# A pad of 32 bytes in front of the row constants of a two-layer attention and feed-forward kernel

## What is computed

```python
x = x + L0_attn(layernorm(x))   # 16 heads, linear attention with phi = silu + 1:
                                # kv = phi(k)^T v per head, out = phi(q) kv, then Wo
x = x + L0_ffn(layernorm(x))    # ternary weights w1, w2, h1, h2, w3 with a scale per output:
                                # h = silu(x w1) * (x w2); h = gelu(h h1); h = gelu(h h2); h w3
x = x + L1_attn(layernorm(x))   # one head over 256 features, softmax over 512 keys
x = x + L1_ffn(layernorm(x))    # tanh(x weight aux1 aux2 + bias)
```

## Time and profile before

| | |
|---|---|
| median of 3 runs | 1983.38 us |
| span of the profiled execution | 1981.5 us, granted TensorE clock 0.996 on the mean |
| PE busy (matmul) | 1961.9 us, 99%, 15288 matmuls |
| VectorE busy | 1289.0 us, 65% |
| ScalarE busy | 1020.0 us, 51% |
| GpSimd busy | 406.8 us, 21% |
| DMA | 46.03 MB, nearly all in the first 100 us |

### The profile page before, as it was taken

One profiled execution on the slowest core, in us unless ns is written; L12 is line 12 of the kernel. 1 busy time (PEld: TensorE's weight loads), 2 busy tenths in 40 slices (PEclk: granted clock), 3 DMA queues, 4 the chain that ended last, 5 costly groups with the idle time before them and its releaser, 6 DMA issues.

```text
span 1981.5 us, 37810 instructions
## 1 busy us (share of the span) xinstructions
PE 1961.9 (99%) x15288; PEld 1895.6 (96%) x15288; DVE 1289.0 (65%) x3292; ACT 1020.0 (51%) x1786; POOL 406.8 (21%) x344
## 2 busy tenths in 40 slices
PE   8999999999999999999999999999999999999998
PEld 7999999999999999999999999999999999999996
DVE  6546768566685665767667676666856667676357
ACT  3445545555554655455554455555546454554433
POOL 1112212212122021311213121121220213112121
PEclk9999999999999999999999999999999999999999
DMA  9600000000000000000000000000000000000000
GB/s 359 224 3 1 22 1 12 11 2 22 1 22 1 1 22 1 22 1 1 22 1 22 1 1 22 1 22 1 23 1 1 22 1 12 1 1 12 1 1 23
DMA packets 24538, 46.03 MB, mean 23 GB/s; under 512 B 1264, under 2 KB 21488, under 8 KB 24176
## 3 DMA queue, kind: packets, MB, share of 16 engines
q1 hardware_dynamic: 24352, 43.41, 6.1%
HBM read 35.02 MB, written 19.92 MB: 28 GB/s over the span
## 4 chain that ended last, share of the span: by engine, by line
PE 97%; DMA 1%; DVE 1%; SPq 1%; issue 0%; ACT 0%; POOL 0%; DVEq 0%; ACTq 0%
PE ffn_fill L1117 49%; PE att_fill L1048 25%; PE ffn_fill L1048 13%; PE ffn_fill L1174 6%; PE att_fill L1136 1%; PE att_fill L1252 1%; DMA scratch_w2T<-in_w2T 1%; DMA w<-scratch_w1T 0%; SPq L543 0%; PE ffn_fill L1285 0%; DVE late_sm L869 0%; PE ffn_fill L1280 0%; ACT late_kv_b L1009 0%; DVE st L671 0%; DVE late_prob_t_lo L864 0%
## 5 line engine op out<-in xcount | busy, mean ns | idle before, releaser
L1117 PE MATMUL ffn_fill<-act_hi,h 128*128 128x256 f32 x4096 | 987.2, 283 | 0.8 <-issue 0.2
L1117 PE MATMUL ffn_fill<-act_lo,h 128*128 128x256 f32 x4096 | 978.2, 280 | 1.2 <-issue 1.2
L1117 PEld LDWEIGHTS ffn_fill<-act_hi,h 128*128 128x128 f32 x4096 | 770.3, 188 | 9.2 <-POOL act_lo L649 3.9
L1117 PEld LDWEIGHTS ffn_fill<-act_lo,h 128*128 128x128 f32 x4096 | 773.1, 189 | 3.6
L976 ACT ACTIVATE whole<-ffn_fill,scales 128x256 f32<-128x256 f32 x512 | 214.0, 469 | 291.3 <-PE ffn_fill L1117 290.1
L649 POOL TENSOR_TENSOR act_lo<-whole,act_hi 128x512 fp32r<-128x512 f32 x128 | 166.8, 1303 | 492.4 <-DVE act_hi L798 492.4
L802 DVE TENSOR_TENSOR act_lo<-whole,act_hi 128x512 fp32r<-128x512 f32 x256 | 183.4, 716 | 112.0 <-ACT act_hi L980 109.7
L1048 PE MATMUL ffn_fill<-half_hi,w 128*128 128x256 f32 x1024 | 245.9, 283 | 0.0
L1048 PE MATMUL ffn_fill<-half_lo,w 128*128 128x256 f32 x1024 | 244.3, 281 | 0.0
L1048 PEld LDWEIGHTS ffn_fill<-half_lo,w 128*128 128x128 f32 x1024 | 193.3, 189 | 0.1
L1048 PEld LDWEIGHTS ffn_fill<-half_hi,w 128*128 128x128 f32 x1024 | 192.5, 188 | 0.4 <-issue 0.2
(11 more groups left out here) (239 smaller groups left out, 3277.8 us busy)
## 6 DMA issues: line engine op xcount, KB each, us to landing
x<-in_L_attn_x SPq DMA_DIRECT2D x16, 512.0 KB, 3.3
out<-x SPq DMA_DIRECT2D x15, 512.0 KB, 2.9
h<-scratch_h1T SPq DMA_DIRECT2D x2, 2048.0 KB, 13.1
h<-scratch_h2T SPq DMA_DIRECT2D x2, 2048.0 KB, 13.4
w<-scratch_w1T SPq DMA_DIRECT2D x1, 1024.0 KB, 7.8
w<-scratch_w2T SPq DMA_DIRECT2D x1, 1024.0 KB, 9.8
w<-scratch_w3T SPq DMA_DIRECT2D x1, 1024.0 KB, 8.3
rows<-in_rows SPq DMA_DIRECT2D x1, 640.0 KB, 5.5
```

The costliest lines, as they stand in the source:

```text
L1117: last = pe.matmul(two(bank)[:, o, :], view(w), view(moving[:, k, :]), start=k == 0 and o == 0 and half == 0, stop=k == KH - 1 and half == ...
```

## The change

One line is added in build, between z_bias and rows: a tile of 8 float32 elements per partition that nothing reads or writes. It moves rows and every tile allocated after it by 32 bytes. The tiles before it and those named late_ stay where they are. No instruction and no wait changes, apart from the addresses.

```diff
@@ -333,6 +333,7 @@
         cols = sb("cols", [P, 4, KD])
         scaled_bq = sb("scaled_bq", [P, KD])
         z_bias = sb("z_bias", [P, KD + 1])
+        sb("row_pad", [P, 8])
         rows = sb("rows", [P, 6, D])
         bv_row, bo_row, s3_row, bout_row, fb_row, u_row = (rows[:, r, :] for r in range(6))
         ident = sb("ident", [P, P])
```

## The result

The changed kernel takes 1999.73 us (median of 4 runs, 1998.59 to 2001.92) where the one before takes 1983.61 us beside it: a ratio of 1.0085 (95% interval 1.0072 to 1.0097): slower by less than 1%, and clear of the noise. The forecast was 1998.8 us. The profiled execution has a span of 1996.2 us, 14.7 us more than before.

What follows compares the result with a forecast made beforehand. TensorE was taken to bound the kernel, matmul count times start-to-start distance. 12.6 + 3.2 + 1.4 - 1.8 = +15.4 us gave a 1996.9 us span and a 1998.8 us median (+0.8%); range 1980 to 2008, the forecast's own 1994 to 2005.4.

Steps and rivals of the forecast that it cites:

- Nothing waits: Steady loop: PE busy 120.58 of 120.60 us, so time is the number of matmuls times their start-to-start distance.
- Even or odd by itself changes nothing, the distance does: Matmul pairs: both odd and both even settle at 120.0 ns; the distance between stationary and moving tile sets the pace.
- the pad brings all pairs to distance 0: All pairs: distance 0 is dearer with 256 columns (120 settled against 116.7 to 118.4 ns), cheaper with 512.
- distance 32 (mod 64): Weights against data: before the pad all such pairs were counted as one distance, 32 modulo 64, going to 0.
- first rival: FFN matmuls load each weight tile twice, so nothing carries over to them: 1983.4 us, up to +4.6 us; 14%.
- 256 bytes modulo 512: With the pad, data lie 256 bytes off the weights modulo 512; FFN could fall to 116.9 ns: -15.4 us, 1968 us; 6%.
- Step 1: FFN matmuls with weights stationary: 10240, 77% settled, from 118.4 to 120.0 ns, +12.6 us.
- Step 2: W (L1174): 1024 matmuls from 116.9 to 120.0 ns, +3.2 us.
- Step 3: wvo and wf against xt: 360 matmuls each from 116.7 to 118.7 ns on average, as short runs, +1.4 us.
- Step 4: 512-column matmuls of wkv, wz and wq: 756 from 233.3 to 230.9 ns, -1.8 us.
- Step 5: Data against data (values, m_parts, xt against qz): distance unchanged, 0; fp32 transposes and late_ pairs also 0.
- Steps 6 and 7: VectorE, ScalarE and POOL: unchanged or hidden under PE, 0; DMAs: 0, ends -0.5 to +0.5 us in the first 35 us.

Runs made afterwards that it cites:

- second block kernel: Against the original kernel: FFN and attention tiles both shifted, aiming at 112 bytes modulo 128 (0 for 512-column pairs); 1973.2 us, ratio 0.9947.
- last kernel: The block kernel with FFN and attention tiles both moved, its places reset modulo 256 (act, xn and what follows 128 bytes further); 1944.6 us, ratio 0.9800 against the original.

## Why the prediction was right, point by point

- What bounds the kernel: right. PE is busy for 121.73 of 121.73 us in a turn, and the changes of the paces show in the time. "Nothing waits" in the loop was too strong: seven FFN distances in a turn are 200 ns and more.
- "Even or odd by itself changes nothing, the distance does": right, shown by moving the weights too (2002.2 and 1983.6 us). The comparison of wvo against xt with wvo against late_xt, on which it rested, was a fair one.
- The distance counted modulo 64, and "the pad brings all pairs to distance 0": right for this pad and wrong as a rule. The period is 256, and it was chance that 32 bytes led from 224 to 256, that is 0. Had the pad been 96 bytes, the same reasoning would have given a loss where 18 us are won. The place of the mistake is the sentence on "distance 32 (mod 64)", in which 32 and 224 fell together although the rows told them apart by 1.5 ns, which I saw and, in the first rival, took only as a sign that something acts on the FFN too. What I wrote on 256 bytes modulo 512 was a worry about a real thing at the wrong place: 256 is one full period.
- The steps can be set against a sum over all starts of PE: every distance goes to the pair of its first matmul, and the differences of the two profiled executions add up to the 15.0 us by which the last matmul starts later.
- Step 1, the FFN, +12.6 us: mechanism right, size too small; it came to +14.5. I took 77% as settled, and nearly all are: the pieces of attention in between stand at distance 0 too and keep the pace, as m_parts against qz at 120.0 from the first matmul on shows. The pace gives 10240 x (119.8 - 118.2) = +16.4 us; the some 115 distances of over 150 ns became 2.3 us shorter together. With all tiles odd, at the same distance 0, they kept their length and the FFN came to +16.7, so those 2.3 us can be the execution and not the change.
- Step 2, W, +3.2: +3.4. Right.
- Step 3, wvo and wf, +1.4: they settle at once as well, and it came to +2.2.
- Step 4, 512 columns, -1.8: wkv 228.2, wz 229.0 and wq 230.3 instead of 233.3, 233.2 and 233.7; it came to -3.6.
- Step 5, data against data, and the rest, 0: data against data came to -0.3, all others to -1.1, most of it in longer distances between the late_ pairs of the last item.
- Steps 6 and 7, the other engines and DMAs, 0: right as to the engines (ScalarE 1020.0 us in both), and nothing shows against it for the DMAs.
- So 14.5 + 3.4 + 2.2 - 3.6 - 0.3 - 1.1 makes 15.1 (15.0 before rounding), and the span grew by 14.7. The forecast's 15.4 is nearer than its parts, and that is luck: the FFN, wvo and wf were put 2.7 us too low, the pairs with 512 columns and the rest 3.2 us too high.
- The rule of the Trainium skill ("TensorE: Matmul & The Clock Gate", Step-by-step: what each phase is for), that loading the next weights takes no read bandwidth from the running matmul, doesn't agree with these runs: by it the place of the stationary tile should make no difference to a matmul whose moving tile stays where it is, and 32 bytes of it make the pace 120.0 or 118.3 ns. The Trainium skill ("TensorE: Matmul & The Clock Gate", Back-to-back issue gap) gives N / 2.4 + 2.5 ns for a matmul that stands alone; by that formula 256 columns would take an estimated 109.2 ns, and no steady pace of float32r matmuls with 256 columns here came under 113.3.

Shown: that the loss of this change comes from the distance between the stationary and the moving tile, which went to 0; and that this distance changes the pace in the full kernel and alone, with 0 and 256 alike and 0 and 128 unlike. Shown too: that it doesn't set the pace alone, since the way in picks one of two paces at 64 and others. Argued only: that the two reads collide in SBUF. Not shown: that the width of the load as such has a part, as the rows of the output change with it. Open: what exactly collides; why W of the second block kernel, at 112, went at 120.0; and why 128 gives 118.6 in the full kernel and 120.0 alone.

## What to carry to other kernels

Where PE is busy without a gap, take the distance from start to start of matmuls from the timeline, for each pair of tiles, and set it beside the distance of the pair's addresses modulo 256: tiles of one kernel that stand at different distances are a free experiment. A neat layout that brings all pairs to distance 0 is a poor choice for float32r matmuls with 256 columns (120.0 ns), and 112 bytes between the stationary and the moving tile was the best one found for the FFN, wvo and m_parts (114.5 to 114.9 ns in the last kernel), though not for W (120.0); with 512 columns distance 0 is best (226.7 ns against 233.3). A pad that moves all tiles behind it changes many pairs at once, so settle the distances pair by pair, and measure: some places have two paces, and a pair's pace can depend on what runs ahead of it.

## What the runs showed of the hardware that I had not expected

- The paces repeat with 256 bytes, as far as it was tried: 226.7 ns at 0 and 256, 232.3 at 128 (512 columns, alone).
- A stream of matmuls can have two steady paces at one distance, and the way in picks one: 117.8 or 113.3 ns at 64, 120.0 or 130.0 at 104, and in the full kernel 117.4 or 120.0 at 160. It keeps it over a run of 112 matmuls (117.8, with 96 bytes).
- The pace does not fall steadily with the width of the stationary tile: 120.0, 116.0, 113.3, 117.8 ns for 128, 96, 64 and 32 columns at distance 0 (the rows of the output change with it).
- Two pages of the profile with the same number of instructions and the same busy share of PE (99%) can be 55 us apart (1999.7 and 1944.6 us); PE has 97% and 93% of their last chains.
